# Layer statistics of the WKV branch as narrow products with a DRAM round trip, and its quarters every 24 steps

## The chip, the cores and the metric

One NeuronCore of a Trainium2 chip. The metric is the device time of one execution in microseconds. The kernel is written engine by engine, with semaphores set by hand: TensorE (PE), VectorE (DVE), ScalarE (ACT), GpSimd (POOL), and SyncE (SP) for most of the transfers.

## What is computed

An input `x` of [2, 1024, 128] is normalised over its 128 channels, and two blocks are added to it: an RWKV block (a recurrence over time with running maximum, sum and weighted sum, then a second layer norm and a channel mix) and an attention block with 16 heads of 8 channels, whose weights are a dense matrix plus two chosen low-rank experts per batch.

```python
xn = _layernorm(x)
x = x + attn_ref(xn, ...) + ffn_ref(xn, ...)

# attn_ref: h = layer_norm(xn); k, v, r from h mixed with its shift
p = jnp.maximum(pp, u + kk); e1 = jnp.exp(pp - p); e2 = jnp.exp(u + kk - p)
y = (e1 * aa + e2 * vv) / (e1 + e2)
p2 = jnp.maximum(pp + w, w + kk)                 # running state aa, bb, pp
x = x + r * y
h2 = layer_norm(x, ln2_g, ln2_b); hp2 = shift(h2)
ck = h2 * cmix_k + hp2 * (1 - cmix_k); cr = h2 * cmix_r + hp2 * (1 - cmix_r)
x = x + sigmoid(cr @ w_cr) * (square(relu(ck @ w_ck)) @ w_cv)

# ffn_ref: q, k, v by svd_moe (dense + top-2 experts)
attn = softmax(einsum('bhsd,bhtd->bhst', q, k)); ctx = einsum('bhst,bhtd->bhsd', attn, v)
out = svd_moe(ctx, ...)
```

## The kernel before

After an opening of some 65 us (norms, gates, the experts folded into effective weights, transposes, the first projections) one long loop runs over 16 head pairs `p` and 8 key tiles, 128 steps in all; `now = p * KEY_TILES + step` is the number of a step. In each step TensorE does, in this order:

- two "places" (`fill_place`, L1388): score products of a later head pair, 512 columns into one PSUM bank, of which VectorE takes the maximum (`read_place`, L1198). Two more places follow behind the scores. Three banks take turns as places (the ring).
- the scores of this step (L1485), two halves of two heads. ScalarE turns each half into exponentials (`exps`, L985), before anything else that it has in the step.
- the value products (L1498) of the step before, from these exponentials.
- the jobs of the step (`product`, L1449): products of the RWKV branch, which take a bank of the same ring. The bank of a job must have been read before the second pair of places of the next step may use it (`released`). Each job is four column groups of 32 output rows, in two passes of fp32, so eight records.

Places run out in step 117; from there VectorE has no maxima.

The RWKV branch is worked in four quarters `q` of 256 time steps for both batches, so in tiles of 128x512. Each engine has a function `branch(t, q)`, which is called in each step with `t = now - q * GAP`, a later quarter first; `GAP` is 26. So the work of a step comes behind the step's own work on VectorE and ScalarE. On GpSimd nothing else ties it to the step: it goes through its list as fast as the semaphores let it. What the steps `t` hold before:

- 1: GpSimd carries the ends of the running states and copies the quarter's window of k, gate, v and x into `quarter_in` (L656, L659).
- 2, 3: running-maximum scans on VectorE, one per batch (L1144). 4 to 7: GpSimd's differences d1, d2, d3 (L665 to L668); 5, 6: their exponentials on ScalarE (L939). 9, 10: running-sum scans, VectorE. 12: logarithm, ScalarE. 13, 14: four clips, GpSimd (L643). 14 to 17: four weights, ScalarE (L946). 16: both accumulator scans, VectorE.
- 18 to 22: numerator, denominator and division on GpSimd and ScalarE, which end in `x1` (L702).
- 26: product "mean" of x1 with `mean_w` (all 1/128), which puts the mean over the channels on all 128 rows; VectorE subtracts it (L1162). 27: square, GpSimd (L706). 28: product "var"; ScalarE's logarithm and, in 29, exponential make the reciprocal deviation `rs2` of 128x512 (L956, L960).
- 31 to 34: h2, its shift difference and the mixes (L715 to L726). 35: product "cr"; 36 to 39: "ck0" to "ck3", with ScalarE's relu (L974) and GpSimd's square (L731); 42: "cv", four products in one, 16 column groups. VectorE multiplies its result with the gate (L1167), and GpSimd adds it to x1 (L739) and the bias to x (L743).

Other work has fixed steps: the late projections of k, v and gate (`LATE_JOBS`, products of 128 columns of weights), the turn of the next pair's maxima in key tile 5 (`split_max` on GpSimd, `turn_max` on TensorE, `copy_turned` on ScalarE), the copy of a pair's context in key tile 0 (L991), and SP's transfers of the next pairs, from key tile 1 on.

## Time and profile before

| | |
|---|---|
| median of three runs | 442.88 us (442.63 to 442.93) |
| the profiled execution | 443.83 us |
| its span on the core | 441.7 us |
| TensorE busy | 423.2 us (96%) |
| VectorE busy | 382.5 us (87%) |
| ScalarE busy | 341.7 us (77%) |
| GpSimd busy | 191.6 us (43%) |

The span is the time between the first and the last event on the core; the execution has some time around it. Busy shares are averages over the opening, the loop with places, and the tail without. Which engine sets the time of a step is read from the step.

### The profile page before, as it was taken

Reading aid. Unit: us, or ns where it says so; the run is one execution under the profiler, and the core shown is the slowest. Engines: PE = TensorE matmul, PEld = TensorE weight load, DVE = VectorE, ACT = ScalarE, POOL = GpSimd, SP = SyncE. Lnnn points to the kernel's source line nnn. Section 1 sums busy time; section 2 is a strip of 40 time slices with the busy share of each in tenths; the row PEclk is TensorE's granted clock in tenths of the full one; section 3 lists DMA queues with packets and bytes.
Section 4 is the critical chain, followed back from the end, with each engine's and each line's share of the span. In section 5 each row is a group of like instructions: output and inputs, shape, how many; then the busy total and the mean of one; then the engine's idle time right before and its main releaser. Section 6 shows DMA issues by size and latency. Waiting matters only on the chain.

```text
span 441.7 us, 8603 instructions
## 1 busy us (share of the span) xinstructions
PE 423.2 (96%) x3266; PEld 146.3 (33%) x3266; DVE 382.5 (87%) x657; ACT 341.7 (77%) x466; POOL 191.6 (43%) x271
## 2 busy tenths in 40 slices
PE   1999989999999999999999999999999999999997
PEld 1744222334233222233223322323333332332335
DVE  8469899998999998799999789999978998978182
ACT  3447837879887898788799869878986987898572
POOL 5039681935551625382352537506363620423200
PEclk9999999999999999999999999999999999999999
DMA  6004403141414151404242422333332322050311
GB/s 242 12 7 54 48 7 33 20 67 19 64 22 68 19 67 17 65 9 68 24 62 22 64 23 46 40 53 32 52 36 25 54 26 45 3 130 5 108 47 50
DMA packets 45797, 20.46 MB, mean 46 GB/s; under 512 B 36828, under 2 KB 37500, under 8 KB 45756
## 3 DMA queue, kind: packets, MB, share of 16 engines
q1 hardware_dynamic: 44630, 18.96, 27.7%
q10 hardware_dynamic: 1126, 0.95, 0.6%
q8 instruction: 26, 0.43, 0.4%
q14 instruction: 15, 0.12, 0.1%
HBM read 4.74 MB, written 4.98 MB: 22 GB/s over the span
## 4 chain that ended last, share of the span: by engine, by line
PE 87%; DVE 8%; ACT 3%; issue 1%; DMA 1%; DVEq 0%
PE banks L1498 27%; PE banks L1485 22%; PE banks L1388 18%; PE banks L1449 8%; DVE half_max L1198 5%; PE banks L1349 3%; ACT probs L985 2%; PE banks L1245 1%; PE banks L1428 1%; PE banks L1355 1%; PE banks L1284 1%; PE banks L1436 1%; PE banks L1341 1%; PE banks L1250 1%; DVE stats L1044 1%
## 5 line engine op out<-in xcount | busy, mean ns | idle before, releaser
L1198 DVE TENSOR_REDUCE half_max<-banks 128x1 f32<-128x512 f32 x512 | 318.4, 683 | 19.0 <-PE banks L1388 17.2
L985 ACT ACTIVATE probs<-banks 128x1024 f32<-128x1024 f32 x256 | 248.2, 1023 | 51.5 <-PE banks L1485 48.3
L1498 PE MATMUL banks<-probs,v_op 128*32 128x512 f32 x1024 | 136.4, 605 | 0.0
L1388 PE MATMUL banks<-k_main,q_main 64*128 64x512 bf16 x512 | 117.0, 384 | 5.1 <-DVE half_max L1198 3.3
L1485 PE MATMUL banks<-q_main,k_main 64*128 64x512 bf16 x512 | 99.3, 377 | 0.4 <-ACT probs L985 0.2
L1485 PE MATMUL banks<-q_tail,k_tail 35*128 35x512 bf16 x512 | 99.3, 377 | 0.0
L1388 PEld LDWEIGHTS banks<-k_main,q_main 64*128 64x128 bf16 x512 | 36.7, 93 | 150.2 <-DVE half_max L1198 131.9
L1485 PEld LDWEIGHTS banks<-q_tail,k_tail 35*128 35x128 bf16 x512 | 27.1, 94 | 26.2
L1485 PEld LDWEIGHTS banks<-q_main,k_main 64*128 64x128 bf16 x512 | 26.4, 95 | 25.1 <-ACT probs L985 10.2
L1498 PEld LDWEIGHTS banks<-probs,v_op 128*32 128x32 f32 x1024 | 20.1, 108 | 31.3 <-issue 30.3
L731 POOL TENSOR_TENSOR work<-work 128x512 f32<-128x512 f32 x16 | 16.7, 1041 | 28.6 <-ACT work L974 28.6
L1449 PE MATMUL banks<-hT,mat_sb 128*32 128x512 f32 x160 | 20.9, 592 | 0.0
L726 POOL TENSOR_TENSOR hT<-hT,run 128x512 f32<-128x512 f32 x8 | 9.5, 1193 | 18.5 <-ACT hT L963 18.5
L633 POOL CAST max_op<-max_left 128x16 bf16<-128x16 f32 x16 | 3.2, 198 | 32.9 <-DVE max_left L1203 32.7
L665 POOL TENSOR_TENSOR work<-run 128x512 f32<-128x512 f32 x4 | 4.2, 1041 | 29.0 <-DVE run L1144 29.0
L739 POOL TENSOR_TENSOR RT<-hT,xn_tok 128x256 f32<-128x256 f32 x8 | 5.7, 740 | 21.7 <-DVE xn_tok L1167 21.7
L1449 PE MATMUL banks<-work,mat_sb 128*32 128x512 f32 x128 | 14.5, 592 | 0.0
L706 POOL TENSOR_TENSOR hT<-hT 128x512 f32<-128x512 f32 x4 | 4.2, 1041 | 21.8 <-DVE hT L1162 21.8
L1178 DVE RECIPROCAL parts<-parts 128x512 f32<-128x512 f32 (+1 forms) x4 | 13.3, 3338 | 0.2 <-DMA parts<-ctx_dram 0.2
L1250 PE MATMUL banks<-ident,xn_tok 128*128 128x128 f32 x16 | 4.3, 433 | 9.1 <-DVE xn_tok L1037 9.1
L974 ACT ACTIVATE work<-banks 128x512 f32<-128x512 f32 x16 | 9.6, 599 | 4.3 <-PE banks L1449 4.3
L1167 DVE TENSOR_TENSOR xn_tok<-banks,xn_tok 128x512 f32<-128x512 f32 x4 | 2.8, 692 | 10.7 <-PE banks L1449 10.7
(186 smaller groups left out, 422.3 us busy)
## 6 DMA issues: line engine op xcount, KB each, us to landing
ctx_dram<-ctx_sb SPq DMA_DIRECT2D x15, 256.0 KB, 2.0
q_main<-parts SPq DMA_DIRECT2D x60, 48.0 KB
k_main<-parts SPq DMA_DIRECT2D x60, 48.0 KB
mat_sb<-in_mats_dram SPq DMA_DIRECT2D x2, 768.0 KB, 5.2
v_op<-V SPq DMA_DIRECT2D x16, 64.0 KB, 3.9
parts<-ctx_dram SPq DMA_DIRECT2D x4, 256.0 KB, 4.4
q_main<-parts SPq DMA_DIRECT2D x30, 32.0 KB
k_main<-parts SPq DMA_DIRECT2D x30, 32.0 KB
```

Of the source, the lines that this page charges most:

```text
L726: g.tensor_tensor(mix_in[i][:, :, :], mix_in[i][:, :, :], h2[:, :, 0:QT], ALU.add).then_inc(mixed, 1)
L731: g.tensor_tensor(kk[i][:, :, :], kk[i][:, :, :], kk[i][:, :, :], ALU.mult).then_inc(kk_ready, 1)
L974: a.activation(flat(kk[i]), ring_bank(ring.index(("job", f"ck{i}", q))), ACT.Relu).then_inc(relu_ready, 1)
L985: a.activation(probs[:, (2 * step + h) % 4, :, :], banks[:, 2 * h:2 * h + 2, :], ACT.Exp).then_inc(b_read, 1)
L1178: v.reciprocal(den_T[0:rows, n, :], den_T[0:rows, n, :]).then_inc(recip_ready, 1)
L1198: v.tensor_reduce(half_max[:, n % 2, u:u + 1], ring_bank(at), axis=AX.X, op=ALU.max).then_inc(a_read, 1)
L1250: last = nc.tensor.transpose(token_tiles(bank(n))[:, k, :], xn_tok[:, 4 * n + k, :], ident[:, :])
L1349: mm(dst, mat("t" + "kvr"[m % 3]), mix_slot[m], start=True, stop=True).then_inc(kvr_ps, 1)
L1388: mm(dst, q_main[HALF * e:HALF * (e + 1), s, P * c:P * c + P], k_main[HALF * e:HALF * (e + 1), s, CHUNK * h:CHUNK * h + CHUNK], start=True ...
L1449: last = mm(dst[g:g + 32, :], weights[:, g:g + 32], moving, start=start, stop=stop)
L1485: last = mm(bank(2 * h + e), k_rows[HALF * e:HALF * e + used, at, P * step:P * step + P], q_rows[HALF * e:HALF * e + used, at, CHUNK * h:C ...
L1498: last = mm(banks[g:g + 32, PV_BANK, :], v_op[:, s % 2, step, e, :], probs[:, (2 * step + h) % 4, e, :], start=(step == 0), stop=True, ski ...
```

## The change

1. The products "mean" and "var" no longer put the same number on all 128 output rows. Each takes 32 equal columns of `mean_w` as weights and, for each of the four row groups, another 128 of the 512 columns as moving data, so that 128 columns run where 512 did. ScalarE copies the mean into `row_stats` (one row of each group matters), and makes the reciprocal deviation there in 128x128. A transfer issued by ScalarE stores the four rows in DRAM (`store_stats`), and another two steps later loads them, spread to all partitions, into `wide_stats` of 128x512 (`load_stats`).
2. The subtraction of the mean and the product with the gate go from VectorE to GpSimd; ScalarE first copies the result of "cv" out of its bank (`gx_kept`).
3. The window copies are gone: every reader takes its quarter from the whole tensor. `x1` has two buffers.
4. `GAP` is 24. For quarters 1 to 3 the recurrence starts ahead of the quarter's own steps: maxima at -6 and -5, d1 and d2 at -4 and -3, exponentials and both sum scans at -1. The logarithm is at 8, clips at 9 and 10, weights at 10 to 13, the accumulator scans at 16 and 17. Quarter 0 keeps its former steps up to 18. The later parts of every quarter stand later: x1 at 25, "mean" 26, "var" 31, "cr" 39, "ck" 40 to 43, "cv" 47.
5. The last late value product and what follows it move by one step.

```diff
-GAP = 26
+GAP = 24
+FIRST_AT = {"max_ends": 1, "max": (2, 3), "exponents": (4, 4), "decays": (5, 6), "sum_ends": 1, "sum": (9, 10), "log": 12,
+            "clip": 13, "weights": 14, "ev": 16, "acc": (16, 16), "den": 18}
+LATER_AT = {"max_ends": -10, "max": (-6, -5), "exponents": (-4, -3), "decays": (-1, -1), "sum_ends": -4, "sum": (-1, -1), "log": 8,
+            "clip": 9, "weights": 10, "ev": 13, "acc": (16, 17), "den": 14}
-PRODUCT_STEP = {"mean": 26, "var": 28, "cr": 35, "ck0": 36, "ck1": 37, "ck2": 38, "ck3": 39, "cv": 42}
+PRODUCT_STEP = {"mean": 26, "var": 31, "cr": 39, "ck0": 40, "ck1": 41, "ck2": 42, "ck3": 43, "cv": 47}
-LATE_JOBS = {2: ("mixed", 9), 3: ("mixed", 10), 9: ("mixed", 11), 10: ("values", 2), 15: ("values", 3)}
+LATE_JOBS = {2: ("mixed", 9), 3: ("mixed", 10), 9: ("mixed", 11), 10: ("values", 2), 16: ("values", 3)}
...
# TensorE
+                def means_of(moving):
+                    for g in range(0, P, 32):
+                        last = mm(dst[g:g + 32, 0:P], mean_w[:, 0:32], moving[:, 4 * g:4 * g + P], start=True, stop=True)
+                    return last
-                    columns(mean_w, flat(x1)).then_inc(mean2_ps, 1)
+                    means_of(flat(x1[q % 2])).then_inc(mean2_ps, 1)
-                    columns(mean_w, flat(sq2)).then_inc(var2_ps, 1)
+                    means_of(flat(sq2)).then_inc(var2_ps, 1)
...
# ScalarE
+            def store_stats(i):
+                act.dma_start(stat_dram[i], row_stats[0:P:32, :]).then_inc(stat_out, 16)
+            def load_stats(i):
+                act.wait_ge(stat_out, 16 * (i + 1))
+                act.dma_start(wide_stats[:, :], bass.AP(stat_dram.tensor, i * CHUNK, [[0, P], [1, CHUNK]])
+                              ).then_inc(stat_in, 16)
+                if t == PRODUCT_STEP["mean"]:
+                    act.wait_ge(mean2_ps, q + 1)
+                    a.copy(row_stats[:, :], ring_bank(ring.index(("job", "mean", q)))[:, 0:P]).then_inc(mean_kept, 1)
+                    act.wait_ge(mean_kept, q + 1)
+                    store_stats(2 * q)
+                if t == PRODUCT_STEP["mean"] + 2:
+                    if q > 0:
+                        act.wait_ge(h2_hat, q)
+                    load_stats(2 * q)
                 if t == PRODUCT_STEP["var"]:
                     act.wait_ge(var2_ps, q + 1)
-                    a.activation(flat(rs2), ring_bank(ring.index(("job", "var", q))), ACT.Ln, bias=eps_c[:, 0:1]
-                                 ).then_inc(log_var_q, 1)
-                if t == PRODUCT_STEP["var"] + 1:
+                    a.activation(row_stats[:, :], ring_bank(ring.index(("job", "var", q)))[:, 0:P], ACT.Ln,
+                                 bias=eps_c[:, 0:1]).then_inc(log_var_q, 1)
                     act.wait_ge(log_var_q, q + 1)
-                    a.activation(rs2[:, :, :], rs2[:, :, :], ACT.Exp, scale=-0.5).then_inc(rs2_ready, 1)
+                    a.activation(row_stats[:, :], row_stats[:, :], ACT.Exp, scale=-0.5).then_inc(rs2_rows, 1)
+                    act.wait_ge(rs2_rows, q + 1)
+                    store_stats(2 * q + 1)
+                if t == PRODUCT_STEP["var"] + 2:
+                    act.wait_ge(centred2, q + 1)
+                    load_stats(2 * q + 1)
+                if t == PRODUCT_STEP["cv"]:
+                    act.wait_ge(cv_ps, q + 1)
+                    a.copy(flat(xc2), ring_bank(ring.index(("job", "cv", q)))).then_inc(gx_kept, 1)
...
# VectorE
-                if t == PRODUCT_STEP["mean"]:
-                    dve.wait_ge(mean2_ps, q + 1)
-                    v.tensor_tensor(flat(xc2), flat(x1), ring_bank(ring.index(("job", "mean", q))), ALU.subtract
-                                    ).then_inc(centred2, 1)
-                if t == PRODUCT_STEP["cv"]:
...
-                    v.tensor_tensor(flat(gx), ring_bank(ring.index(("job", "cv", q))), flat(ecr), ALU.mult
-                                    ).then_inc(gated, 1)
...
# GpSimd
-                    for window, whole in ((k_q, k_of), (gate_q, gate_of), (v_q, v_of), (x_q, xnT[:, :, :])):
-                        g.tensor_copy(window[:, :, :], whole[:, :, bass.ds(q * QT, QT)]).then_inc(windows, 1)
...
+                if t == PRODUCT_STEP["var"] - 1:
+                    pool.wait_ge(stat_in, 32 * q + 16)
+                    g.tensor_tensor(flat(xc2), flat(x1[q % 2]), wide_stats[:, :], ALU.subtract).then_inc(centred2, 1)
                     pool.wait_ge(centred2, q + 1)
                     g.tensor_tensor(sq2[:, :, :], xc2[:, :, :], xc2[:, :, :], ALU.mult).then_inc(squared2, 1)
...
                 if t == PRODUCT_STEP["cv"] + 1:
+                    pool.wait_ge(gx_kept, q + 1)
+                    pool.wait_ge(cr_ready, q + 1)
+                    g.tensor_tensor(gx[:, :, :], xc2[:, :, :], ecr[:, :, :], ALU.mult).then_inc(gated, 1)
```

VectorE from the sum scans of quarter 0 to the next quarter's, before. The scans are the rows with `run`; those that read `quarter_in` and `col_sb` are running maxima, those with `xn_tok` sums, those with `work,run,quarter_in` accumulators; L1162 subtracts the mean.

```order
L1144 SCALAR_TENSOR_TENSOR run<-work,run,quarter_in 128x256 x2
L1198 TENSOR_REDUCE half_max<-banks 128x1 x14
L1203 TENSOR_REDUCE max_left<-half_max 128x16
L1198 TENSOR_REDUCE half_max<-banks 128x1 x26
L1162 TENSOR_TENSOR hT<-hT,banks 128x512
L1198 TENSOR_REDUCE half_max<-banks 128x1 x6
L1203 TENSOR_REDUCE max_left<-half_max 128x16
L1198 TENSOR_REDUCE half_max<-banks 128x1 x2
L1144 SCALAR_TENSOR_TENSOR run<-quarter_in,run,col_sb 128x256
```

The same place on VectorE now; maxima read `kept_k`, accumulators `work,run`.

```order
L1199 SCALAR_TENSOR_TENSOR run<-work,run 128x256 x2
L1247 TENSOR_REDUCE half_max<-banks 128x1 x8
L1199 SCALAR_TENSOR_TENSOR run<-kept_k,run,col_sb 128x256
L1247 TENSOR_REDUCE half_max<-banks 128x1 x4
L1199 SCALAR_TENSOR_TENSOR run<-kept_k,run,col_sb 128x256
L1247 TENSOR_REDUCE half_max<-banks 128x1 x2
L1252 TENSOR_REDUCE max_left<-half_max 128x16
L1247 TENSOR_REDUCE half_max<-banks 128x1 x14
L1199 SCALAR_TENSOR_TENSOR run<-work,run,xn_tok 128x256 x2
```

Quarter 1's maxima moved from behind the mean of quarter 0 to two and three steps behind the accumulators of quarter 0, both sum scans follow four steps later in one place, and the subtraction is gone.

GpSimd from the first reader of quarter 1's accumulators' weights to its denominator, before: L739 and L743 are the residual and bias adds behind cv of quarter 0, L687 the denominator of quarter 1.

```order
L643 TENSOR_SCALAR xn_tok<-work,col_sb 128x512
L731 TENSOR_TENSOR work<-work 128x512
L683 TENSOR_TENSOR quarter_in<-work,quarter_in 128x512
L739 TENSOR_TENSOR RT<-hT,xn_tok 128x64x4 x2
L743 TENSOR_TENSOR x_sb<-x_sb,vb_ob 128x512
L687 TENSOR_TENSOR xn_tok<-work,xn_tok 128x512
```

The same adds on GpSimd now (L765, L769): L759 is the gate product that was VectorE's, L721 and L723 make quarter 1's x1.

```order
L714 TENSOR_TENSOR xn_tok<-xn_tok,work 128x512
L717 TENSOR_TENSOR xn_tok<-xn_tok,kept_gate 128x512
L759 TENSOR_TENSOR xn_tok<-hT,xn_tok 128x512
L765 TENSOR_TENSOR RT<-hT,xn_tok 128x64x4 x2
L769 TENSOR_TENSOR x_sb<-x_sb,vb_ob 128x512
L665 TENSOR_TENSOR run<-run,zero_c 128x2
L721 TENSOR_TENSOR xn_tok<-xn_tok 128x512
L723 TENSOR_TENSOR hT<-xn_tok,xnT 128x512
```

The work behind cv of one quarter now stands directly ahead of the next quarter's x1.

ScalarE around the mean and var of quarter 0 now (L1040 the exponentials of the scores, L977 those of quarter 1's differences, L995, L1004 and L1007 on `row_stats`, L1046 the context copy, L980 quarter 1's logarithm).

```order
L977 ACTIVATE work<-work,col_sb 128x512
L977 ACTIVATE xn_tok<-work,col_sb 128x512
L1040 ACTIVATE probs<-banks 128x1024 x2
L1046 COPY ctx_sb<-banks 128x512
L992 ACTIVATE xn_tok<-xn_tok 128x512
L1040 ACTIVATE probs<-banks 128x1024 x4
L995 COPY row_stats<-banks 128x128
L960 DMA stat_dram<-row_stats 4x128
L1040 ACTIVATE probs<-banks 128x1024 x4
L965 DMA wide_stats<-stat_dram 128x512
L1040 ACTIVATE probs<-banks 128x1024 x2
```

Between the mean's exponentials of the scores there was no other work on ScalarE; now a copy and two DMA issues stand there, and quarter 1's two exponentials stand in one step.

## Rows read from the trace of the kernel before

**Rows 1.** The page, part 1: engine, busy us, share of the span, instructions.

```profile
PE 423.2 (96%) x3266; PEld 146.3 (33%) x3266; DVE 382.5 (87%) x657; ACT 341.7 (77%) x466; POOL 191.6 (43%) x271
```

The columns of the next group are: stretch in us from the span's start, its length, busy time (instructions) of TensorE, its weight loads, VectorE, ScalarE and GpSimd, granted clock, DMA share, GB/s.

**Rows 2.** Busy time by stretch, steps 15, 16, 23, 26, 28, 29, 33, 42, 116.

```profile
106.64:110.21 3.57, 3.57 (x29) 1.72 (x29) 2.48 (x5) 3.04 (x5) 1.66 (x2) 1.00 0.46 52
110.21:113.89 3.68, 2.79 (x22) 0.75 (x21) 3.68 (x7) 3.68 (x6) 0.85 (x1) 1.00 0.46 101
128.99:131.48 2.49, 2.49 (x22) 0.76 (x22) 2.49 (x5) 1.94 (x3) 2.10 (x4) 1.00 0.45 52
136.45:140.10 3.65, 3.64 (x29) 1.01 (x29) 3.08 (x6) 2.24 (x4) 0.89 (x1) 1.00 0.54 51
...
142.59:145.94 3.35, 3.35 (x30) 1.01 (x29) 3.32 (x7) 2.63 (x4) 0.83 (x4) 1.00 0.07 13
145.94:148.97 3.03, 2.84 (x25) 0.86 (x24) 3.03 (x6) 3.03 (x6) 0.88 (x1) 1.00 0.00 0
156.43:158.99 2.56, 2.56 (x21) 0.67 (x20) 2.56 (x5) 2.56 (x4) 0.12 (x1) 1.00 0.57 142
183.23:189.53 6.30, 6.22 (x55) 1.79 (x53) 4.38 (x8) 3.13 (x5) 1.95 (x3) 1.00 0.51 48
...
398.06:400.89 2.83, 2.83 (x26) 0.73 (x24) 2.79 (x3) 2.45 (x4) 1.66 (x6) 1.00 0.02 4
```

**Rows 3.** Timeline behind the mean product: start, us, engine, work, idle and releaser.

```profile
138.44 0.69 DVE L1162 TENSOR_TENSOR hT<-hT,banks 128x512 f32<-128x512 f32 x1 [0.57 <-PE banks L1449]
...
139.78 0.09 PEld L1388 LDWEIGHTS banks<-k_main,q_main 64*128 64x128 bf16 x1 [0.50 <-DVE half_max L1198]
```

**Rows 4.** The chain that ended last: start, us, a cv product, and the last spread.

```profile
184.29 3.48 PE banks L1449 x32
...
433.79 0.99 PE banks L1542 x16
```

**Rows 5.** Timeline behind cv of quarter 0, and x1 of quarter 0 (125.90, 127.26).

```profile
125.90 1.27 POOL L700 TENSOR_TENSOR xn_tok<-xn_tok 128x512 f32<-128x512 f32 x1 [2.85 <-ACT xn_tok L953]
127.26 1.27 POOL L702 TENSOR_TENSOR hT<-xn_tok,quarter_in 128x512 f32<-128x512 f32 x1
...
187.87 0.69 DVE L1167 TENSOR_TENSOR xn_tok<-banks,xn_tok 128x512 f32<-128x512 f32 x1 [1.92 <-PE banks L1449]
...
188.64 1.43 POOL L739 TENSOR_TENSOR RT<-hT,xn_tok 128x256 f32<-128x256 f32 x2 [4.35 <-DVE xn_tok L1167]
...
190.02 1.28 POOL L743 TENSOR_TENSOR x_sb<-x_sb,vb_ob 128x512 f32<-128x512 f32 x1
```

**Rows 6.** Timeline, VectorE: the two accumulator scans of quarter 0 in step 16.

```profile
111.55 1.39 DVE L1144 TENSOR_TENSOR_SCAN run<-work,run,quarter_in 128x256 f32<-128x256 f32 x2
112.85 8.72 DVE L1198 TENSOR_REDUCE half_max<-banks 128x1 f32<-128x512 f32 x14
```

**Rows 7.** Timeline, ScalarE in step 16, and a weight load in step 33.

```profile
109.59 1.94 ACT L985 ACTIVATE probs<-banks 128x1024 f32<-128x1024 f32 x2 [0.17 <-PE banks L1485]
111.41 0.59 ACT L991 COPY ctx_sb<-banks 128x512 f32<-128x512 f32 x1
111.88 0.74 ACT L946 ACTIVATE work<-work,neg_first 128x512 f32<-128x512 f32 x1
...
158.23 0.10 PEld L1485 LDWEIGHTS banks<-q_main,k_main 64*128 64x128 bf16 x2 [0.48 <-ACT probs L985]
```

**Rows 8.** Timeline: ScalarE's DMA issue (ACTq) and its idle time behind another.

```profile
10.14 0.20 ACT L805 ACTIVATE qb_s<-col_sb 128x1 f32<-128x1 f32 x1 [0.20 <-issue]
...
57.10 0.65 ACTq L927 DMA_DIRECT2D q_tail<-max_rows  x1
```

**Rows 9.** DMA issues: names, issues, KB each, us from issue to landing.

```profile
ctx_dram<-ctx_sb SPq DMA_DIRECT2D x15, 256.0 KB, 2.0
...
parts<-ctx_dram SPq DMA_DIRECT2D x4, 256.0 KB, 4.4
...
vb_ob<-in_rows_dram ACTq DMA_DIRECT2D x1, 128.0 KB, 3.2
```

159 lines of the change are left out of this document (88 added, 71 removed).

## Prediction

> **What bounds the kernel now.** I read the page's busy shares first, then cut the long loop at the starts of its value products, and last looked at single waits. TensorE is busy 96% of the span, VectorE 87%, ScalarE 77% [rows 1]. "Step n" below is the n-th of the 128 key-tile steps; its row in [rows 2] runs from the value products issued in it to the next ones, so it holds the products listed for step n. A plain step (23) takes 2.49 us with both TensorE and VectorE at 2.49: VectorE's four maxima of 0.62 fill it exactly, and TensorE has next to nothing spare. So whatever either of the two gets on top lengthens the step, unless the other is longer in the same step. The steps with more say what things cost: var (28) 3.35, so a product of 512 columns costs 0.86; mean (26) 3.65, so 1.16; cv (42) 6.30; one scan in a step without product (29) 3.03, so 0.54, with TensorE idle; the bare pair of scans (16) 3.68, so 1.19 [rows 2]. The reader is to see in the last two that TensorE's column is shorter than the stretch, and VectorE's is all of it. The granted clock is 1.00 throughout, so the clock gives and takes nothing.
>
> **Small products.** One product of 512 columns takes 3.48/4 = 0.87 in cv; the last spread takes 0.99 for two rounds of eight records with 256 columns, 0.50 each [rows 4]. A line through both gives 0.31 for 128 columns. Bounds: 0.22, a quarter of 0.87, and 0.50, if eight records never go faster than in the spread. I take 0.31, in between, because 0.50 to 0.87 is already less than proportional. No var step has other cover, so four times 0.86 - 0.31 = -2.2.
> In a mean step VectorE also subtracts (0.69), and the next place then waits 0.50 for it [rows 3]; that is what lies between 1.16 and 0.86. The subtraction goes to GpSimd, so the mean saves 1.16 - 0.31: four times, -3.4.
> VectorE's gate product behind cv (0.69 [rows 5]) delays the next maximum likewise: 6.30 - 2.49 - 3.48 [rows 2, 4] leaves 0.33, of which I take 0.27 for it. ScalarE's copy of 0.59 [rows 7] takes its place and frees the bank no later. Three times (the last cv stands where no maxima are left): -0.8.
>
> **Running maxima and sums on VectorE.** Two scans take 1.30 from start to start of the next work [rows 6]. Before, one maximum scan of quarters 1, 2 and 3 lies bare (steps 29, 55, 81): 3 x 0.54. In quarters 2 and 3 they now lie with the ck2 and ck3 products (steps 42, 43, 66, 67), whose 0.86 covers 0.65: -1.6. The accumulator scans of quarter 0 stood in step 16, the value product of 1.08 in 15: 1.08 + 1.19 [rows 2]. Now both are in 16, where the longer, 1.30, counts: -1.0.
> Quarter 1 has no quarter before the last one to hide behind. Its maxima stand in steps 18 and 19 without a product: 0.54 + 0.65 = +1.2. Its sum scans stand in step 23 and wait there for two exponentials that ScalarE runs after those of the scores. I count from the start of the step's value products, V, in step 16 at 110.21 [rows 2]. The scores' exponentials end at V + 1.20 (111.41 [rows 7]), the two of 0.74, overlapping by 0.1, at V + 2.6, the scans (1.30) at V + 3.9, while VectorE is free at V + 1.34 (111.55 [rows 6]). Less 0.1 of slack: +2.45, bounds 1.2 (no wait, scans alone) and 2.7. In steps 47 and 71 the same wait is under cv's 3.5 us and costs nothing.
>
> **GpSimd.** The four window copies per quarter go, all of them off the path. What matters is its chain behind cv, since before, x1 was ready four steps ahead of the mean, and now one. From the moment when cv's result can be read (187.87 [rows 5]): ScalarE's copy 0.6, hand-over 0.1, gate product 1.28, hand-over 0.1, the two residual adds 1.43, the bias add 1.28, a carry of some 0.1, then the multiply and x1, 1.36 and 1.27 [rows 5]: 7.5. The value products came 1.66 after that moment (189.53), without the 0.33 they would at 1.3; two plain steps and 0.99 later, at 7.3, the mean product of the next quarter could start, its weights about 0.4 sooner. This wait is new, 0.5 each in steps 50, 74 and 98: +1.5, bounds 0 and 3. The second tight place is cr (steps 39, 63, 87): denominator, numerator and the first mix add now stand between ScalarE's last weight and the product, three times 1.2 to 1.3 in less than two steps: +0.4, bounds 0 and 1.5.
>
> **ScalarE.** A plain step leaves it 2.49 - 1.83 = 0.66, since its two exponentials of the scores take 1.82 from start to start [rows 7]; I use 1.83. It gets per quarter: two small reads of a bank and one small exponential (bounds 0.20, one column [rows 8], and 0.74 [rows 7]; I take 0.26, nearest to the small one), the copy after cv (hidden), and four DMA issues. An issue lasts 0.65 [rows 8], and ScalarE was seen idle for 0.20 behind one; I take 0.5, bounds 0.2 and 0.65. The heaviest stretch is steps 31 to 38: var's 1.1, then context copy and logarithm 1.0, a load 0.5, four weights 2.3, two mixes 1.2 and a turned copy, 6.3 us against 8 x 0.66 + 0.31 = 5.6; the backlog ends near 0.7. Such a backlog showed once as a wait of 0.48 for the scores' bank in step 33 [rows 7], which still took only 2.56 [rows 2], because VectorE was the bound. I take +0.5 in all, bounds 0 and 3. Queued behind ScalarE's waits are always the next scores, for which TensorE's value products wait.
>
> **The DMA round trip.** Each mean and each rstd row goes to DRAM and comes back spread over 128 partitions. Stores have two steps before the load, against 2.0 us to landing [rows 9]: hidden. The load of the mean is issued behind the scores at V + 1.2 of step 28; the var product wants its weights about V + 0.45 in step 31, so 7.9 after that V, and GpSimd needs at most 2 x 1.28 [rows 5] for subtraction and square, less since the square reads one tensor; I take 2.4. So it may land up to 7.9 - 1.2 - 2.4 = 4.3 us after issue. The rstd load (step 33) is wanted by products from step 39 on and by the split of maxima behind it in GpSimd's queue in step 37; it has more room and sets nothing first. Landings of a spread load were 3.2 (128 KB) and 4.4 (256 KB, several at once, from DRAM) [rows 9]. This one is 256 KB and alone: I take 3.7, no wait. SP's queue gets nothing new. In the tail the products stand two steps earlier, in steps that still have places; a product costs its 0.86 there too (2.83 in step 116, where 1.97 is left without it [rows 2]): +0.1.
>
> **Sum.** Gains 3.4 + 2.2 + 0.8 + 1.6 + 1.0 = 9.0. Costs 1.2 + 2.45 + 1.5 + 0.4 + 0.5 + 0.1 = 6.15. Net -2.9 on a span of 441.7: 438.8. The profiled execution took 443.83, 2.1 more than its span, so 440.9; the median of the three runs is 442.88, 0.95 below it, so 440.0.
>
> **Rivals.** (1) The waits that I counted on GpSimd and ScalarE mostly don't occur: x1 in time, the maxima's slack hiding the rest, small products at 0.22. Then 2.4 + 0.7 less: 437 to 439. For it: GpSimd is busy 43% only. Against it: the chain after cv has no gap to close. Chance 0.20. (2) Small products are bound by their eight records: 0.50 each, +1.5, 441.5. Chance 0.12. The Trainium skill, "TensorE: Matmul & The Clock Gate", section "Back-to-back issue gap", gives about 81 ns for each pair of weight load and matmul at 128 columns in a stream; with eight pairs that would be an estimated 0.65 a product and 442.7 in all. No row here has this form, and 62 ns per record in the spread speaks for less. (3) Slower: the spread load lands late. Price: from 4.3 us on every microsecond of latency costs one in each quarter, since the var product stands in TensorE's queue ahead of the next scores. At 5.3 it is 4 x 1.0: 440.0 becomes 444.0, and more where the rstd load is late too. It decides from 4.3 + 2.9/4 = 5.0 us on, where the kernel is as slow as before. For it: the 4.4, and that SP's transfers of the next pairs may reach into these steps. Against it: the DMA share near step 29 is 0.00 [rows 2]. Chance 0.12. The Trainium skill, "DMA: Bandwidth & Descriptors", section "Anatomy of one DMA", has about 2.0 us fixed and bytes over 436 GB/s, so an estimated 2.6 us here, in time by 1.7; the 2.0 of the stores agrees. (4) Hardly a change: GpSimd's and ScalarE's new waits at their upper bounds, +3 over the sum, 442 to 443.7. Chance 0.12.
>
> **Chances.** Forecast 0.44. A measurement of this kernel can tell about 0.2% (0.9 us) from no change. Below 442.0: forecast, (1), (2): 0.76. Within: (4), 0.12. Above 443.8: (3), 0.12. The range 437.2 to 443.3 leaves out (3) and the end of (1).
>
> **What would show it.** Mean and var stretches at 2.8 (quarters 1 to 3: mean at 3.3, with TensorE waiting for GpSimd's x1). Steps 29, 55, 81 at 2.49. Steps 18 and 19 at 3.0 and 3.1, and step 23 near 4.9 with VectorE waiting for ScalarE's exponentials. Cv at 6.0. Landings of the spread load under 4.3 and no wait of TensorE on the square. It is wrong if ScalarE's scores start late by more than 0.7 in the steps from 31 on, or if a mean product still takes above 0.5.

## The result, and the profile after

The changed kernel takes 445.60 us (median of five executions, 444.48 to 445.80) against 442.93 us (442.63 to 444.52) for the kernel before, timed beside it. The ratio is 1.0046, with a 95% interval of 1.0026 to 1.0065: it is slower by 0.5%. The forecast was 440.0, so both its sign and its range (437.2 to 443.3) were wrong. The profiled execution took 445.75, with a span of 443.6 against 441.7. Of these 1.9 us, 0.4 lie in the opening, which varies from execution to execution (see the end); from the start of step 1 to the end of the loop it is 366.34 against 364.87, so 1.5 us or 0.3% of the whole.

Each experiment below was timed beside the kernel before, and there it took 444.06 to 444.23 us (medians of 13 to 32 executions), against 442.93 here. So ratios of different experiments can be held against each other to some 0.3% only, and single parts are read from the steps.

First the page's busy times of the kernel after, to be held against [rows 1]: engine, busy us, share of the span, instructions.

```profile
PE 420.7 (95%) x3265; PEld 148.6 (34%) x3266; DVE 378.7 (85%) x649; ACT 341.7 (77%) x474; POOL 194.0 (44%) x271
```

TensorE does 2.5 us less and VectorE 3.8 us less than before, and the span is 1.9 us longer all the same. The time did not go into work. It went into waits and into a slower clock, and those one finds by cutting the loop into steps. The next view has stretches of the kernel after in the form of [rows 2]: steps 16, 18, 19, 23, 24, 26 (mean), 31 (var), 33, 37, 47 (cv), 50 (mean of quarter 1) and 127. Columns: stretch, length, busy time (instructions) of TensorE, its weight loads, VectorE, ScalarE and GpSimd, granted clock, DMA share, GB/s.

```profile
109.56:113.23 3.67, 3.67 (x29) 1.72 (x28) 3.67 (x7) 3.61 (x6) 1.41 (x2) 1.00 0.56 97
115.72:119.14 3.42, 2.78 (x21) 0.75 (x20) 3.42 (x6) 2.87 (x4) 2.46 (x3) 1.00 0.62 50
119.14:122.18 3.04, 2.80 (x22) 0.76 (x21) 3.04 (x6) 2.07 (x4) 0.88 (x1) 1.00 0.23 27
129.81:134.79 4.98, 2.79 (x21) 0.75 (x20) 3.77 (x7) 4.36 (x6) 0.00 (x0) 1.00 0.43 46
134.79:138.81 4.02, 4.02 (x22) 0.88 (x21) 2.71 (x5) 2.28 (x4) 1.26 (x1) 0.58 0.21 70
141.29:144.18 2.89, 2.89 (x30) 1.02 (x29) 2.67 (x6) 2.14 (x4) 0.00 (x0) 1.00 0.62 51
154.30:157.19 2.89, 2.89 (x30) 1.36 (x29) 2.67 (x6) 2.25 (x5) 0.00 (x0) 1.00 0.45 48
159.69:162.52 2.83, 2.57 (x23) 0.63 (x21) 2.69 (x5) 2.83 (x5) 2.41 (x3) 1.00 0.55 190
170.10:172.80 2.70, 2.61 (x24) 0.86 (x24) 2.65 (x6) 2.70 (x6) 1.06 (x3) 1.00 0.03 6
199.76:205.68 5.92, 5.92 (x54) 1.79 (x53) 3.88 (x7) 3.74 (x6) 0.69 (x1) 1.00 0.37 42
210.65:213.72 3.07, 2.91 (x30) 0.94 (x28) 2.48 (x5) 2.11 (x4) 1.08 (x1) 1.00 0.49 49
430.36:433.99 3.63, 2.13 (x19) 1.13 (x17) 2.39 (x3) 1.38 (x2) 0.00 (x0) 1.00 0.09 34
```

A step is read by asking which engine's busy time equals its length. In step 23 none does: TensorE 2.79, VectorE 3.77 and ScalarE 4.36 of 4.98, so there the engines wait for each other. In step 24 TensorE is busy all 4.02 us, with as many matmuls as in any plain step, at a granted clock of 0.58. In steps 33 and 37 (and in 38, of 2.59) it is ScalarE's column that reaches the length. In step 127 nothing does.

All 128 steps, cut so in both traces, give the account. A product is counted as what its step has over a plain step in the same place of a pair. The change after minus before, in us:

| part | forecast | measured |
|---|---|---|
| opening, to the start of step 1 | 0 | +0.4 |
| steps 15 and 16 | -1.0 | -1.1 |
| steps 18 and 19, bare maxima | +1.2 | +1.5 |
| step 23, sum scans wait | +2.45 | +2.5 |
| step 24, slower clock | none | +1.5 |
| four means, with the wait for x1 | -3.4 + 1.5 | -2.5 |
| four vars | -2.2 | -1.7 |
| maxima of steps 29, 55, 81 | -1.6 | -1.6 |
| three cvs | -0.8 | -1.0 |
| wait ahead of cr | +0.4 | 0 |
| ScalarE's backlog (33, 37, 38 and their like) | +0.5 | +1.7 |
| tail, steps 111 to 118 and 122 to 126 | +0.1 | +0.1 |
| steps 119 to 121 | none | +0.35 |
| step 127 | none | +1.5 |

With +0.1 of small differences this is the +1.9 of the spans. Most terms were close. Three rows that the forecast did not have, steps 24, 119 to 121 and 127, are 3.4 of the 4.8 us between -2.9 and +1.9. The next two sections show that they have two causes.

### The profile page after: what moved, and what is told of

Its sections match the earlier page's. It is cut to its first block, busy times and chain, and to the rows that moved or that the text cites. A ratio compares the mean times of both kernels' runs of the same rounds, so it can differ in the third digit from the quotient of the medians.

```text
span 443.6 us, 8631 instructions
## 1 busy us (share of the span) xinstructions
PE 420.7 (95%) x3265; PEld 148.6 (34%) x3266; DVE 378.7 (85%) x649; ACT 341.7 (77%) x474; POOL 194.0 (44%) x271
## 4 chain that ended last, share of the span: by engine, by line
PE 75%; DVE 8%; ACT 7%; issue 3%; POOL 3%; DMA 2%; SPq 1%; ACTq 0%; POOLq 0%; DVEq 0%
PE banks L1552 23%; PE banks L1539 19%; PE banks L1437 15%; PE banks L1498 7%; ACT probs L1040 4%; DVE half_max L1247 4%; PE banks L1398 3%; DVE parts L1227 1%; PE banks L1294 1%; PE banks L1404 1%; DMA parts<-ctx_dram 1%; PE banks L1333 1%; PE banks L1390 1%; PE banks L1299 1%; DVE stats L1099 1%
## 5 line engine op out<-in xcount | busy, mean ns | idle before, releaser
L1040 ACT ACTIVATE probs<-banks 128x1024 f32<-128x1024 f32 x256 | 247.8, 1024 | 40.3 <-PE banks L1539 37.3
L1539 PE MATMUL banks<-q_main,k_main 64*128 64x512 bf16 x512 | 101.7, 379 | 1.3 <-ACT probs L1040 0.9
L1539 PE MATMUL banks<-q_tail,k_tail 35*128 35x512 bf16 x512 | 101.6, 379 | 0.0
L1539 PEld LDWEIGHTS banks<-q_main,k_main 64*128 64x128 bf16 x512 | 27.4, 95 | 29.7 <-ACT probs L1040 17.0
L1539 PEld LDWEIGHTS banks<-q_tail,k_tail 35*128 35x128 bf16 x512 | 29.0, 95 | 22.9 <-issue 0.6
L759 POOL TENSOR_TENSOR xn_tok<-hT,xn_tok 128x512 f32<-128x512 f32 x4 | 5.1, 1273 | 29.9 <-ACT hT L1030 29.9
L695 POOL TENSOR_TENSOR work<-work,xn_tok 128x512 f32<-128x512 f32 x4 | 5.1, 1276 | 20.3 <-ACT xn_tok L980 20.3
L1046 ACT COPY ctx_sb<-banks 128x512 f32<-128x512 f32 x15 | 8.9, 592 | 2.1 <-PE banks L1552 2.1
```

What stands on the lines that cost most here:

```text
L1040: a.activation(probs[:, (2 * step + h) % 4, :, :], banks[:, 2 * h:2 * h + 2, :], ACT.Exp).then_inc(b_read, 1)
L1046: a.copy(ctx_sb[:, s % 2, :], bank(PV_BANK)).then_inc(ctx_copied, 1)
L1539: last = mm(bank(2 * h + e), k_rows[HALF * e:HALF * e + used, at, P * step:P * step + P], q_rows[HALF * e:HALF * e + used, at, CHUNK * h:C ...
```

## The last step: a product ahead of the context copy

The view is the timeline of the kernel after (start, us, engine, work, idle and releaser), from the context copy of pair 14 to the wait behind the loop.

```profile
413.04 0.59 ACT L1046 COPY ctx_sb<-banks 128x512 f32<-128x512 f32 x1
...
416.64 1.84 SPq L511 DMA_DIRECT2D parts<-ctx_dram  x1
...
423.57 3.35 DVE L1227 RECIPROCAL parts<-parts 112x512 f32<-112x512 f32 x1 [3.66 <-DMA parts<-ctx_dram]
...
432.11 0.67 DVE L1239 TENSOR_TENSOR x_sb<-x_sb,banks 128x512 f32<-128x512 f32 x1
...
432.93 1.13 PE L1477 MATMUL banks<-ident,RT 128*128 128x128 f32 x8 [1.50 <-DVE x_sb L1239]
```

It is one chain: the copy, the store, four loads, VectorE's two reciprocals, and behind them in VectorE's queue the addition for which TensorE waits 1.50 us at the end of the loop. The same places before were these.

```profile
409.59 0.59 ACT L991 COPY ctx_sb<-banks 128x512 f32<-128x512 f32 x1
...
419.78 3.35 DVE L1178 RECIPROCAL parts<-parts 112x512 f32<-112x512 f32 x1 [0.24 <-DMA parts<-ctx_dram]
...
428.38 0.69 DVE L1190 TENSOR_TENSOR x_sb<-x_sb,banks 128x512 f32<-128x512 f32 x1
...
430.99 1.16 PE L1428 MATMUL banks<-ident,RT 128*128 128x128 f32 x8
```

The copy comes 3.45 us later (3.44 counted from the start of step 119), as long as a cv product. The copy needs pair 14's last value products, which TensorE issues in step 120. The last cv stood behind them in step 120; now it stands in step 119, ahead of them. How much room the chain had is read at its end and not in the middle: VectorE waited 0.24 us for the loads before too, but its addition was done at 429.07, and TensorE came to the product that needs it at 430.99, without a wait. With the 0.15 that lies between the two now (432.78 and 432.93), that was room for 1.8 us. Against it the addition now comes 3.35 us later, counted from the start of step 127: 3.08 are the copy's, and the rest comes with the loads, of which SyncE's second issue took 1.84 us instead of 0.83. What is left over is the 1.5.

**The last cv one step later.** The edit alone:

```diff
+def product_step(name, q):
+    return PRODUCT_STEP[name] + (name == "cv" and q == QUARTERS - 1)
...
-if t == PRODUCT_STEP["cv"]:
+if t == product_step("cv", q):
```

> The changed kernel, with quarter 3's cv product one step later (step 120 instead of 119), that is again behind pair 14's last value products; nothing else is touched. Theory: the 1.5 us that the changed kernel loses in its last step (3.63 against 2.09) come from the context copy of pair 14, which waits behind this cv, and pass through the store, the loads and VectorE's normalisation to the wait of TensorE behind the loop. Then the copy comes some 3.4 us earlier, the last step is back at 2.1, and the kernel takes 1.5 us less than the changed one: 444.1. Rival: VectorE's tail is bound by its own order of work, and the copy's delay is hidden; then the last step stays at 3.6 and the time at 445.6.

Measured: 0.9983 of the kernel before (0.9971 to 0.9994). Against the changed kernel's 1.0046 that is some 2.8 us less, more than the 1.5 expected; what the trace shows of it comes below. Step 127 of this kernel:

```profile
429.42:431.50 2.08, 2.08 (x18) 1.12 (x16) 0.00 (x0) 1.38 (x2) 0.00 (x0) 1.00 0.21 80
```

It is back at 2.08 with TensorE busy all of it. The rival fell. Steps 119 to 121 are back too: together they take 9.59 us, as in the kernel before, and 9.94 in the changed kernel. So the place of this one product cost 1.54 + 0.35 = 1.9 us, not 1.5.

**The same step in the kernel before.** The reverse edit: in the kernel before, the last cv goes from step 120 to 119.

```diff
+return PRODUCT_STEP[name] - (name == "cv" and q == QUARTERS - 1)
```

> The kernel before, with quarter 3's cv product one step earlier (119 instead of 120), ahead of pair 14's last value products, as it stands in the changed kernel; nothing else is touched. Theory: the late context copy alone makes the end longer, whatever else was changed: the last step goes from 2.09 to 3.1 to 3.7, +1.5 us, ratio to the kernel before 1.003. Rival: the kernel before has room there, since its products end later or its normalisation is not the last: the last step stays at 2.1.

Measured: 1.0052 (1.0031 to 1.0072), and this for step 127:

```profile
429.29:433.16 3.87, 2.13 (x19) 1.13 (x17) 2.63 (x3) 1.38 (x2) 0.00 (x0) 1.00 0.08 31
```

Step 127 is 1.8 us longer, and steps 119 to 121 take 9.94 instead of 9.59. So one product placed one step early costs 2.1 us in a kernel that has nothing else of the change. The cause is settled from both sides. In the other kernels with the cv in 119, step 127 took between 2.47 and 3.74. It was 2.47 to 3.09 in the three in which the issue of SyncE's second load took 0.82 us, and 3.54 or more where it took 1.78 to 1.99: that passes through.

## Steps 23 and 24: a wait, and then the clock

Timeline of the kernel after at the two sum scans of quarter 1:

```profile
132.45 1.39 DVE L1199 TENSOR_TENSOR_SCAN run<-work,run,xn_tok 128x256 f32<-128x256 f32 x2 [1.21 <-ACT xn_tok L977]
...
134.48 0.39 PE L1437 MATMUL banks<-k_main,q_main 64*128 64x512 bf16 x1 [2.19 <-DVE half_max L1247]
```

This wait was forecast, and so was its size. What was not: it left TensorE idle for 2.19 us, and then the granted clock fell. Stretches of half a us of the kernel after, where the fall begins and ends:

```profile
135.00:135.50 0.50, 0.50 (x8) 0.00 (x0) 0.50 (x2) 0.00 (x0) 0.00 (x0) 0.89 0.00 0
135.50:136.00 0.50, 0.50 (x4) 0.00 (x0) 0.50 (x2) 0.00 (x0) 0.00 (x0) 0.50 0.00 0
...
139.00:139.50 0.50, 0.50 (x8) 0.00 (x0) 0.50 (x1) 0.50 (x1) 0.50 (x1) 1.00 0.26 33
```

The clock is at 0.50, the 1.2 GHz level, for some 3.4 us, and at 1.00 (2.4 GHz) on both sides. TensorE is the bound there, so the step takes 1.53 us more.

**Sum scans in two other steps.** Quarter 1 gets a row of times of its own:

```diff
+SECOND_AT = {**LATER_AT, "sum": (0, 1)}
...
-return (LATER_AT if q else FIRST_AT)[what]
+return (FIRST_AT, SECOND_AT, LATER_AT, LATER_AT)[q][what]
```

> The changed kernel, with quarter 1's two sum scans in steps 24 and 25, one each, instead of both in step 23 where they wait for ScalarE's exponentials. Theory: step 23's stall of 2.5 us and the fall of TensorE's granted clock in step 24 (0.58, 1.53 us more) both hang on this wait. Then step 23 is 2.49, steps 24 and 25 are some 3.05 and 3.1 (a bare scan each), at clock 1.00: -4.0 + 1.2 = -2.8, 442.8. Rival 1: the clock falls for a reason of its own: -2.5 + 1.2 = -1.3, 444.3. Rival 2: the scans still wait for ScalarE in step 24: less than 1 us is won.

Measured: 0.9971 (0.9961 to 0.9981), with a clock of 1.00 throughout in the profiled execution. Steps 23, 24 and 25 took 2.48, 3.04 and 4.11 instead of 4.98, 4.02 and 2.48: -1.85, not -2.8. The mean clock was 1.000 in 7 of 8 executions. The wait and the slower clock are both gone, as expected. The missing 1.0 is in step 25, where the second scan took 1.83 us (below).

**Zero products.** To part the wait from the clock, TensorE gets something to do in the wait: products with zero weights, added to the bank of the value products.

```diff
 for at in behind:
+    if p * KEY_TILES + step == GAP - 1 and at == behind[-1]:
+        for _ in range(20):
+            mm(banks[0:32, PV_BANK, 0:P], zero_c[:, 0:1].to_broadcast([P, 32]), ident[:, :],
+               start=False, stop=True, skip_group_check=True)
     fill_place(at)
```

> The changed kernel, with 20 products of zero weights (128 columns, added to the bank of the value products, which they leave as it is) on TensorE in step 23, ahead of the matmul that waits for VectorE's maximum. The wait itself stays; only TensorE is busy in it. Theory: the granted clock falls in step 24 because TensorE idled 2.19 us. Then step 23 stays at 4.98, step 24 is back at 2.49 at clock 1.00, and the kernel takes 1.5 us less: 444.1. Rival: the clock falls whatever TensorE does in the wait: 445.6, or more where the 20 products (some 0.1 us each) outlast the wait.

Measured: 1.0034 (1.0021 to 1.0047). This run was badly placed. The wait falls on the places that TensorE fills behind the scores of the next step, so the products stood a step too early and made a stretch of their own:

```profile
127.47:134.68 7.21, 7.21 (x62) 5.04 (x61) 3.31 (x6) 4.48 (x6) 1.36 (x2) 1.00 0.34 38
```

That is 4.72 over a plain step, 0.24 each. But VectorE and ScalarE caught up meanwhile: step 23 took 3.05, step 24 2.49 at full clock, and step 127 2.47, so that 4.7 us more work on TensorE made a span only 0.3 us longer than the changed kernel's. So it does not part the wait from the clock, since the wait went too. It is one more kernel without the idle time (behind step 18 TensorE never stood idle for 0.4 us in the loop), and its mean clock was 1.000 in 11 of 12 executions, 0.999 in the other.

**Zero products in the wait.** The same with `== GAP` and 8 products.

> The changed kernel, with 8 products of zero weights on TensorE directly ahead of the place matmul that idled 2.19 us behind step 23's sum scans (one such product took 0.24 us in the run before this one, where 20 of them stood a step too early). Nothing is taken from the wait. Theory: the granted clock falls to 0.50 for 3.4 us because TensorE stood idle. Then step 23 stays at 5.0, step 24 comes back to 2.49, the mean clock is 1.000, and the kernel takes 1.5 us less than the changed one, 444.1 against 445.6. Rival: the fall has nothing to do with this wait, as step 1 of the kernel with the last cv moved suggests, where it came in the opening: then it comes anyway in most executions, mean clock 0.996, and nothing is won.

Measured: 1.0018 (0.9996 to 1.0041). Timeline and steps 23 and 24 of it:

```profile
132.35 1.93 PE L1570 MATMUL banks<-ident,zero_c 128*32 128x128 f32 x16
134.61 0.39 PE L1437 MATMUL banks<-k_main,q_main 64*128 64x512 bf16 x1 [0.33 <-DVE half_max L1247]
```

```profile
129.94:134.92 4.98, 4.66 (x37) 2.42 (x36) 3.77 (x7) 4.36 (x6) 0.00 (x0) 1.00 0.44 47
134.92:137.41 2.49, 2.49 (x21) 0.76 (x21) 2.49 (x5) 1.36 (x3) 0.10 (x1) 1.00 0.00 0
```

Step 23 is as long as ever, with TensorE busy in 4.66 us of it, and step 24 is back at 2.49 with full clock, as the theory has it. Each execution also comes with its mean granted clock. In the kernels in which TensorE idles in this wait it was below 1.000 in every execution: 5 of 5 of the changed kernel, 12 of 12 with the last cv later, 11 of 11 with later maxima, 12 of 12 with SyncE's issues, and the one with wide products (these three below), 41 of 41. In the changed kernels without the wait (both scans moved, or the 20 zero products) it was less in 4 of 35, and in the kernel before in 7 of 68. With the 8 zero products in the wait it was 1.000 in 7 of 12 (442.1 to 444.0 us) and less in five (444.8 to 447.4); why in so many is open.

The traces say the same of the place. TensorE idled some 2.2 us in step 23 in five of them, and in four of these the granted clock was 0.50 for 3.4 us right behind it, with a step 24 of 4.02 to 4.04. In the eight traces without this idle time no low stretch lies in the loop. Shorter idle stretches were followed by none: 0.89 us in step 16 of the kernel before, 1.25 in step 25 with the sums in two steps, 1.50 and 1.74 in step 127 (the changed kernel, and the kernel before with the early cv).

The fifth trace speaks against a simple tie. In the profiled execution of the kernel with the last cv later, TensorE idled as long in step 23, and step 24 was 2.49 at full clock. The low stretch, also some 3.4 us, lay in the opening:

```profile
65.50:66.00 0.50, 0.50 (x4) 0.30 (x6) 0.50 (x2) 0.41 (x1) 0.00 (x0) 0.66 0.45 49
...
68.06:71.02 2.96, 2.96 (x22) 0.79 (x21) 2.07 (x4) 1.39 (x2) 0.00 (x0) 0.83 0.40 41
135.69:138.18 2.49, 2.49 (x22) 0.75 (x21) 2.49 (x5) 1.36 (x3) 0.10 (x1) 1.00 0.00 0
```

That also adds up to the 2.5 us by which this kernel's span fell: the place of the cv gave 1.9 and step 24 gave 1.5, while the low stretch took 0.47 in step 1 and at most 0.4 ahead of it. What is shown: every execution of a kernel with the idle time of 2.2 us had a mean clock below 1.000, and filling the wait or removing it gave step 24 its full clock in all six traces of such kernels. What stays open: where the low stretch lies in executions that have no trace, and why it was in the opening in one that has.

## Steps 18 and 25: VectorE's scans against GpSimd

A scan of 128x256 alone takes 0.74 us. In three places one took longer. The rows are GpSimd's work and the scan in the kernel after (step 18), then in the one with two steps for the sums (step 25), then in the combined one of the next section with SyncE's issues (step 31).

```profile
116.36 1.28 POOL L709 TENSOR_TENSOR xn_tok<-xn_tok,kept_v 128x512 f32<-128x512 f32 x1
117.05 1.14 DVE L1199 TENSOR_TENSOR_SCAN run<-kept_k,run,col_sb 128x256 f32<-128x256 f32 x1
117.59 0.58 POOL L665 TENSOR_TENSOR run<-run,zero_c 128x2 f32<-128x2 f32 x1
```

```profile
136.66 1.83 DVE L1200 TENSOR_TENSOR_SCAN run<-work,run,xn_tok 128x256 f32<-128x256 f32 x1
136.68 1.27 POOL L724 TENSOR_TENSOR hT<-xn_tok,xnT 128x512 f32<-128x512 f32 x1
```

```profile
149.61 1.28 POOL L725 TENSOR_TENSOR work<-run,kept_k 128x512 f32<-128x512 f32 x1
...
150.42 1.01 DVE L1213 TENSOR_TENSOR_SCAN run<-work,run,xn_tok 128x256 f32<-128x256 f32 x1
```

GpSimd ends at 117.64, 137.95 and 150.89; the scans end at 118.19, 138.49 and 151.43, each 0.54 or 0.55 later. So a scan does not share with GpSimd, it waits for the end of its operation and then has 0.54 us left to do. A fourth meeting, in step 31 of the last kernel below, fits: 0.96 us, with its end 0.55 behind GpSimd's. By that a GpSimd operation that ends in the first 0.2 us of a scan should cost nothing (an estimate, 0.74 - 0.54), and in the kernel before one ended 0.12 us into a scan of step 9, which took 0.74. The first group shows it the other way round too: GpSimd's copy of a few numbers, some 0.2 us otherwise, lasts 0.58 and ends with the scan. VectorE's maxima, which read banks, keep their 0.62 beside GpSimd. The Trainium skill, "SBUF — State Buffer", section "Who interferes with whom", says that a VectorE instruction with two inputs in SBUF contends with a GpSimd instruction that reads SBUF, and that the one that comes second is blocked until the other is through. The trace agrees that one of the two waits for all of the other, with 0.27 to 1.09 us per meeting. On who waits it is less clear: in the second group the scan's row starts 0.02 us ahead of GpSimd's, and still it is the scan that is late. The forecast should have used this rule: the change puts bare scans on the path just where GpSimd has its work.

**Maxima one step later.** `SECOND_AT = {**LATER_AT, "max": (-5, -4)}`.

> The changed kernel, with quarter 1's two maximum scans one step later (19 and 20 instead of 18 and 19). In step 18 of the changed kernel a scan took 1.14 us instead of 0.74 while GpSimd's numerator product ran; in step 20 GpSimd has only a small carry. Theory: the 0.4 us are a collision of the two engines. Then all scans take 0.74, steps 18, 19 and 20 are 2.49, 3.03 and 3.2, and the kernel takes 0.4 us less than the changed one: 445.2. Rival: a scan behind a step's maxima takes 1.14 in its first place whatever GpSimd does, and the steps 19 and 20 are 3.4 and 3.0: no change.

Measured: 1.0019 (1.0009 to 1.0029). Both scans took 0.74, and step 18 was 2.49. But steps 18 to 21 sum up to 11.65, against 11.61 in the changed kernel. Its steps 20 and 21, and a weight load in step 21:

```profile
121.01:124.27 3.26, 2.80 (x22) 1.12 (x21) 3.23 (x7) 2.07 (x3) 0.88 (x1) 1.00 0.04 8
124.27:127.14 2.87, 2.72 (x25) 0.85 (x24) 2.48 (x5) 1.52 (x3) 2.65 (x7) 1.00 0.02 6
```

```profile
125.48 0.10 PEld L1446 LDWEIGHTS banks<-neg_ident,max_op 128*32 128x32 bf16 x3 [1.06 <-POOL max_op L656]
```

The collision is gone, and its gain went into a new wait: the first difference of quarter 1 now runs on GpSimd ahead of the split of the maxima, for which TensorE waits 1.06 us in step 21. The collision was the theory's, the total the rival's. What the whole kernel won came from elsewhere: step 127 took 2.85 instead of 3.63, and the opening was 0.2 shorter.

## ScalarE: are the DMA issues the backlog?

**Issues on SyncE.** ScalarE keeps its copies and exponentials, and SyncE makes the four transfers per quarter, ahead of its loads for the next pairs.

```diff
-act.dma_start(stat_dram[i], row_stats[0:P:32, :]).then_inc(stat_out, 16)
+sp.dma_start(stat_dram[i], row_stats[0:P:32, :]).then_inc(stat_out, 16)
...
-act.dma_start(wide_stats[:, :], bass.AP(stat_dram.tensor, i * CHUNK, [[0, P], [1, CHUNK]])
+sp.dma_start(wide_stats[:, :], bass.AP(stat_dram.tensor, i * CHUNK, [[0, P], [1, CHUNK]])
```

> The changed kernel, with the two stores and two loads of the means and rstds per quarter issued by SyncE instead of ScalarE (SyncE's loads of the next pair's second head stand behind them, as before behind the turned maxima). Theory: the late scores in steps 33, 37, 38 and their like (+0.34, +0.16, +0.11 per quarter) are the backlog of ScalarE, of which its DMA issues (0.50 a store, 0.32 a load) are the part that can go. Then those steps are back at 2.49, 2.61 and 2.49 or near, and the kernel takes 1.8 us less than the changed one: 443.8. Rival: the backlog is made by the weights, copies and mixes themselves; the steps stay within 0.1 and at most 0.5 us is won.

Measured: 1.0007 (0.9993 to 1.0020). Step 33 and its like fell from 2.83 to 2.55; steps 37 and 38 stayed at 2.70 and 2.59. So the issues cost 0.28 three times, 0.85 in all, and the rest is made by the weights, mixes and copies. Half the theory stands. The rival's 0.5 is exceeded too.

Which of the issues it is, the rows of ScalarE tell. First the changed kernel, whose step 31 starts at 154.30, then this one, whose step 31 starts at 154.40:

```profile
156.39 0.50 ACTq L960 DMA_DIRECT2D stat_dram<-row_stats  x1
156.94 1.94 ACT L1040 ACTIVATE probs<-banks 128x1024 f32<-128x1024 f32 x2 [0.57 <-PE banks L1539]
...
159.76 1.04 ACT L1040 ACTIVATE probs<-banks 128x1024 f32<-128x1024 f32 x1
159.78 0.33 ACTq L965 DMA_DIRECT2D wide_stats<-stat_dram  x1
```

```profile
156.73 1.94 ACT L1049 ACTIVATE probs<-banks 128x1024 f32<-128x1024 f32 x2 [0.27 <-PE banks L1548]
...
159.55 4.02 ACT L1049 ACTIVATE probs<-banks 128x1024 f32<-128x1024 f32 x4
```

With the store in its queue, ScalarE starts the next exponentials of the scores 2.64 us after the start of step 31, without it 2.33. From there to the exponentials of step 33 it is 2.82 in both kernels, with no idle time between, and the load stands beside an exponential; the one behind it starts 0.90 later in both kernels. So the cost in step 33 is the store's of step 31, carried along by a full queue, and the load cost nothing here.

**Wide products again.** Mean and var with 512 columns per row group, all else as changed:

```diff
-last = mm(dst[g:g + 32, 0:P], mean_w[:, 0:32], moving[:, 4 * g:4 * g + P], start=True, stop=True)
+last = mm(dst[g:g + 32, :], mean_w[:, 0:32], moving, start=True, stop=True)
```

> The changed kernel, with mean and var products of 512 columns for every 32 rows instead of 128; ScalarE still reads 128 columns, so the means and rstds used are those of other tokens. Theory: a product then costs 0.86 again instead of 0.40: mean stretches 3.35 and var 3.35, so +0.46 in each of eight: 3.7 us more than the changed kernel, 449.3. Rival: the stretches of var are set by ScalarE's reads, not by the product, and var grows by less than 0.3.

Measured in one execution: 448.98 us. Var went from 2.89 to 3.35, as expected, the step behind it from 2.50 to 2.68, and the means from 2.89 to 3.35 in quarter 0 but from 3.07 to 3.69 in quarter 1. In all the small products are worth 4.9 us here, not 3.7: the small ones also give ScalarE room in the next step and shorten the means that wait. Time alone would show less, since this execution's step 1 began 1.6 us earlier than the changed kernel's. The rival fell.

## Putting it together

**Combined.** The last cv in step 120, and for quarter 1:

```diff
+SECOND_AT = {**LATER_AT, "sum": (2, 7), "max": (-5, -4), "exponents": (-3, -3)}
```

> The changed kernel, with the last cv in step 120, quarter 1's sum scans in steps 26 and 31, where a small product stands, and its maximum scans in steps 19 and 20 with both differences of GpSimd behind its split of maxima in step 21. Theory: the end gives 1.5; steps 23 and 24 are both 2.49 at clock 1.00 (-4.0), the scans beside small products cost 0.25 each; steps 18 to 21 are 2.49, 3.03, 3.2 and 2.54 (-0.3). Sum 445.6 - 1.5 - 4.0 + 0.5 - 0.3 = 440.3, 0.6% under the kernel before. Rival: the scans meet GpSimd's work in their new places too and take 1.1 to 1.8 instead of 0.74; then 1 to 2 us come back: 441.5 to 442.5.

Measured: 439.72 us, 0.9906 of the kernel before (0.9889 to 0.9924), with a clock of 1.000 in all six executions. From the start of step 1 to the end of the loop it takes 360.76 us, 4.1 less than the kernel before, so the gain does not hang on the opening. Its steps 23, 24, 25, 26 and 31:

```profile
127.96:130.45 2.49, 2.49 (x22) 0.75 (x21) 2.48 (x5) 2.49 (x5) 0.07 (x1) 1.00 0.42 46
130.45:133.13 2.68, 2.58 (x21) 0.59 (x21) 2.68 (x5) 2.68 (x5) 0.00 (x0) 1.00 0.41 43
133.13:135.96 2.83, 2.58 (x22) 0.63 (x20) 2.60 (x5) 2.83 (x5) 2.41 (x2) 1.00 0.49 122
135.96:138.97 3.01, 3.01 (x31) 1.02 (x29) 2.90 (x5) 1.99 (x4) 0.13 (x1) 1.00 0.50 50
...
149.09:152.12 3.03, 3.03 (x30) 1.35 (x29) 3.03 (x6) 2.39 (x5) 0.00 (x0) 1.00 0.45 49
```

Both sum scans took 0.74 and cost 0.12 and 0.14 under the small products, less than the 0.25 assumed. Steps 18 to 21 gave 0.3. The new cost is in steps 24 and 25, where ScalarE's column reaches the length (+0.19 and +0.35).

**With issues on SyncE.** The two edits together.

> The combined kernel, with its stores and loads of means and rstds issued by SyncE. Theory: as in the changed kernel, that takes 0.28 from each of steps 33, 57 and 81 and nothing elsewhere: -0.7 (step 33 had 2.69 here), 439.0. Rival: SyncE's loads for the next pairs come later behind these and cost as much as is won: 439.7.

Measured: 438.87 us, 0.9881 (0.9864 to 0.9898). Steps 57 and 81 gave 0.28 each and step 33 0.20, but step 31 took 3.30 instead of 3.03: the scan met GpSimd's difference there (the third collision above). Net -0.5 in the trace; the two ratios do not tell it from zero.

**Decays apart.** `"decays": (-1, 1)` in addition, for quarter 1.

> The combined kernel with issues on SyncE, and the second of quarter 1's two decay exponentials in step 25 instead of 23 (the sum scans that read both stand in 26 and 31). Theory: steps 24 and 25 are 2.68 and 2.83 in the combined kernel because ScalarE has both exponentials (1.4 us), the context copy and a logarithm within two steps, and TensorE waits 0.26 and more for the scores. With one moved behind them each is 2.5 to 2.6: -0.4 against the run without this edit, 438.6. Rival: the second one now lands on the mean product's read and on the reciprocal's exponential, and the wait moves to steps 25 and 26 with the same sum: no change.

Measured: 0.9884 (0.9866 to 0.9902). Steps 24 and 25 were 2.49 and 2.48, so the backlog of the two exponentials is gone and did not move on to step 26 (3.03); but step 103 took 0.2 more, and the opening of this execution was 1.3 us longer. From step 1 to the end of the loop it is 0.39 less than without this edit, as the theory has it; the time shows no gain. Step 31 still took 3.25, by the fourth meeting of a scan with GpSimd.

## Why the prediction was wrong, point by point

**What it missed.** (1) Of the tail it said "In the tail the products stand two steps earlier", and priced that by TensorE's columns alone, +0.1. That sum was right for what it covers, steps 111 to 118. But it did not ask what is queued behind a product that is moved past other work: the last cv, which moved by one step. Behind it now stood pair 14's value products, and on them hung the context copy and the longest chain of the tail, which had room for 1.8 us and got 3.35 more. That was +1.54 in step 127 and +0.35 in steps 119 to 121, together +1.9, shown from both sides. (2) It said "The granted clock is 1.00 throughout, so the clock gives and takes nothing." That was read from a kernel whose TensorE idles for 0.89 us at most in the loop. The change made a wait of 2.2 us, which the forecast itself had worked out, and the clock followed: +1.5.

**What it mis-sized.** (3) ScalarE's backlog: +0.5 forecast, +1.7 measured, within the bounds of 0 and 3. It was counted as one sum over eight steps. The steps do not pool their room: 33, 37 and 38 each ran over. Moving the issues took away 0.85 of it, and the rows put that down to the store, 0.28 in each of three quarters. (4) A small product costs 0.40, not 0.31; its eight records run in 0.05 us each:

```profile
142.18 0.40 PE L1503 MATMUL banks<-hT,mean_w 128*32 128x128 f32 x8
```

That is +0.7 over eight products, between the forecast and its second rival of 0.50. The Trainium skill's 81 ns for each pair, "TensorE: Matmul & The Clock Gate", section "Back-to-back issue gap", gave an estimated 0.65; the measurement decides for 0.40. (5) The bare maxima in steps 18 and 19: +1.5 for +1.2, by the collision with GpSimd.

**What was right.** Steps 15 and 16, the maxima of 29, 55 and 81, and above all the wait in step 23 with its place, its cause and its 2.5 us. The wait for x1 is real but 0.18 and 0.19 in two of the quarters and 0.03 in the last, not 0.5: the path through GpSimd had more room. Cr did not wait. The spread loads landed in 3.4 us (3.7 taken), so the third rival, the only one clearly on the slower side, did not happen; the kernel became slower in another way. The estimate of 2.6 us beside that rival was 0.8 too low. The Trainium skill, "DMA: Bandwidth & Descriptors", section "Anatomy of one DMA", gives its figures for transfers that GpSimd issues, and these were issued by ScalarE. Nor did the 2.0 us of the stores agree with it: they move 256 KB too, for which the same estimate is 2.6.

```profile
wide_stats<-stat_dram ACTq DMA_DIRECT2D x8, 256.0 KB, 3.4
```

By this account (1) and (2) cost 3.4 us. Without them the span would have fallen by 1.5 us, an estimate, where the forecast had 2.9: its sign was lost by (1) and (2), and the rest of the error by what was mis-sized.

**The opening.** Its +0.4 is not the change's: among kernels whose opening is the same, step 1 began between 66.06 and 68.06 us, and executions of the kernel before had spans from 440.5 to 443.1. What makes it vary was not looked into. It is why single parts of 0.5 us are read here from steps and not from times.
